# Attention banks, chunk order, spread sums and unread products in a fused two-layer kernel

## What is computed

```
h = concat(mean_over_hidden(x @ W.T + b), txt)           # 64 x 96 x 64
h = h + ssm_stack(ln(h))                                  # 4 state-space layers
h = h + ln_affine(z + moe(z)), z = ln(h)                  # 16 experts, top 2
h = h + attention(ln(h))                                  # 8 heads of 64, strictly causal
h = h + recurrent(ln(h))                                  # 96 steps, one after the other:
    i, f, o = sigmoid(x_t U + h V); g = tanh(...)
    c_new = h * c + i * g;  h_new = o * tanh(c_new)
```

## Time and profile before

| | us |
|---|---|
| three runs, median | 860.01 |
| lowest and highest of them | 848.58, 863.31 |
| the profiled execution, its own time | 853.76 |
| span of its instructions | 852.0 |
| mean granted TensorE clock in it | 0.854 of full |
| state-space part and before | 0 to 234 |
| expert slots 0 to 47, first attention | 234 to 404 |
| expert slots 48 to 95, steps 0 to 31 beside them | 404 to 556 |
| second attention | 556 to 714 |
| exposed steps 32 to 95 | 714 to 850 |

### The profile page before, as it was taken

One profiled execution on the slowest core, in us unless ns is written; L12 is line 12 of the kernel. 1 busy time (PEld: TensorE's weight loads), 2 busy tenths in 40 slices (PEclk: granted clock), 3 DMA queues, 4 the chain that ended last, 5 costly groups with the idle time before them and its releaser, 6 DMA issues.

```text
span 852.0 us, 16446 instructions
## 1 busy us (share of the span) xinstructions
PE 690.1 (81%) x6414; PEld 410.8 (48%) x6414; DVE 531.8 (62%) x1104; ACT 358.7 (42%) x667; POOL 253.6 (30%) x223
## 2 busy tenths in 40 slices
PE   3687888952689999988889999979899888776775
PEld 3674655642532222354234434357577666555554
DVE  3855675569956555375557867479767673556443
ACT  2232444333324455554444455635555434232332
POOL 4256764466400224120331402145223240011000
PEclk9999789866579999999989999979999979555555
DMA  9840000000044434101322222000000000000000
GB/s 185 140 77 10 1 1 2 1 0 1 0 138 132 134 107 140 39 2 33 95 73 79 84 88 79 18 2 2 2 2 2 1 2 5 7 11 7 11 9 12
DMA packets 42402, 36.85 MB, mean 43 GB/s; under 512 B 20888, under 2 KB 29848, under 8 KB 42328
## 3 DMA queue, kind: packets, MB, share of 16 engines
q1 hardware_dynamic: 41242, 35.57, 16.3%
q10 hardware_dynamic: 1088, 0.26, 0.2%
HBM read 33.85 MB, written 1.97 MB: 42 GB/s over the span
## 4 chain that ended last, share of the span: by engine, by line
PE 53%; DVE 25%; ACT 8%; issue 6%; POOL 4%; DMA 2%; SPq 1%; POOLq 0%; DVEq 0%; ACTq 0%
PE PS L1591 9%; PE PS L1578 8%; PE PS L1554 6%; PE PS L1626 3%; PE PS L1674 3%; PE PS L1685 3%; DVE XC L937 3%; PE PS L1605 2%; PE PS L1647 2%; PE PS L1540 2%; PE PS L1658 2%; DVE st L919 2%; DMA BIG<-in_x 2%; ACT Y L672 2%; DVE st L935 2%
## 5 line engine op out<-in xcount | busy, mean ns | idle before, releaser
L1591 PE MATMUL PS<-Y,W1f 64*128 64x512 f32 x384 | 110.1, 653 | 6.0 <-DVE Y L1078 3.9
L1578 PE MATMUL PS<-XC,w2s 128*64 128x512 f32 x384 | 104.1, 622 | 0.0
L1554 PE MATMUL PS<-LS,V 64*64 64x32 f32 x1140 | 70.3, 269 | 40.5 <-DVE LS L1214 40.5
L1554 PEld LDWEIGHTS PS<-LS,V 64*64 64x64 f32 x1140 | 58.3, 186 | 71.6 <-DVE LS L1214 65.2
L717 ACT ACTIVATE XC<-PS 128x1024 f32<-128x1024 f32 x68 | 69.3, 1022 | 54.0 <-PE PS L1578 45.3
L1078 DVE TENSOR_TENSOR Y<-XD,UF 128x512 f32<-128x512 f32 x96 | 64.8, 689 | 15.2 <-DMA UF<-gd 9.2
L574 POOL TENSOR_TENSOR Y<-XC 128x512 f32<-128x512 f32 x12 | 14.7, 1226 | 173.6 <-DVE XC L1058 173.6
L1591 PEld LDWEIGHTS PS<-Y,W1f 64*128 64x128 f32 x384 | 30.1, 188 | 50.9 <-DVE Y L1078 24.9
L1578 PEld LDWEIGHTS PS<-XC,w2s 128*64 128x64 f32 x384 | 19.2, 135 | 73.2 <-issue 62.2
L1201 DVE SCALAR_TENSOR_TENSOR LS<-LS 128x32 f32<-128x32 f32 x96 | 21.4, 222 | 51.3 <-ACT LS L812 39.4
L178 POOL TENSOR_TENSOR st<-st,mhalf 128x8 f32<-128x8 f32 x24 | 39.3, 1639 | 37.0 <-DVE st L922 37.0
(11 more groups left out here) (236 smaller groups left out, 1463.9 us busy)
## 6 DMA issues: line engine op xcount, KB each, us to landing
UF<-gd SPq DMA_DIRECT2D x192, 128.0 KB, 2.9
BIG<-in_x SPq DMA_DIRECT2D x8, 512.0 KB, 12.4
out<-X SPq DMA_DIRECT2D x48, 32.0 KB, 2.0
W1f<-in_L_ffn_w SPq DMA_DIRECT2D x2, 512.0 KB, 5.9
EX<-in_L_ffn_w SPq DMA_DIRECT2D x1, 1024.0 KB, 15.6
H<-in_txt SPq DMA_DIRECT2D x2, 256.0 KB, 12.6
w2s<-in_L_ffn_w SPq DMA_DIRECT2D x1, 512.0 KB, 9.9
gd<-EX SPq DMA_DIRECT2D x6, 64.0 KB, 1.7
```

What stands on the lines that cost most here:

```text
L1554: mm = pe.matmul(PS[r, b, o:o + HN], V3[r, g, :], HB[r, (t - 1) % 4, :], start=False, stop=True, skip_group_check=True)
L1578: mm = pe.matmul(PS[64 * h:64 * h + 64, 6, :], w2s[:, 2 * p + h, :], Hb[:, n % 2 * 2 + h, :], start=(p == 0), stop=(p == E // 2 - 1))
L1591: mm = pe.matmul(PS[:, n % 2 * 2 + h, :], W1f[r, 2 * p + h, :], Rb[r, n % 4, :], start=True, stop=True)
```

## The change

- Second attention: in range 2 the keys are turned into bank 5 (from its second unit on) and all Z go through bank 4, copied by ScalarE alone. `turn_keys` in bank 5 no longer waits for the queries' copies or for bank 7. TensorE's order within a unit changes: `turn_p` comes ahead of `project`, and range 2's two `queries` halves both come behind `gather`. VectorE's chunk work stands behind the unit's `less_max` and copies.
- Chunk 2's settling (all but its first half sum) comes seven slots later; `out` and what follows it one slot later for chunks 0 and 3 to 4. The recurrence and residual chunks 0 and 1 start earlier, by one and two slots.
- Squares go from GpSimd to ScalarE everywhere (TAIL_ACT in the second attention). In chunks 4 and 5 the scaling goes from GpSimd to VectorE.
- In exposed steps a residual chunk's parts are spread over twelve slots (XALONE) and the two sums of a half are parts of their own (r and q). In the second attention chunks 2 and 3 get new unit numbers.
- In each exposed step but the last and the six with `att_out` or `turn_x`, TensorE does one fp32 product of 256, 384, 160 or 256 columns by step number modulo 4, into bank 1. Nothing reads it and it waits for nothing; its operands are expert weights.

```diff
-        TAIL_DVE = {0: (2, 3, 4, 5), 1: (6, 7), 2: (8, 9), 3: (10,), 4: (11, 12), 6: (13, 14)}
-        TAIL_POOL = {0: ("sq0",), 1: ("pw0", "mu0", "ga"), 2: ("sq1",), 4: ("pw1", "mu1")}
+        TAIL_DVE = {0: (2, 3, 4, 5), 1: (6, 7), 2: (8, 9), 3: (10,), 4: (11, 12), 5: (13, 14)}
+        TAIL_POOL = {1: ("pw0", "mu0", "ga"), 4: ("pw1", "mu1")}
+        TAIL_ACT = {1: 0, 4: 1}
...
-        LS0 = 3 * E + 11
+        LS0 = 3 * E + 10
...
-                     sq1=9, k11=10, k12=10, pw1=10, mu1=11, out=12, t0=13, t1=13, k13=13, k14=13)
-
-        XB = (3 * E + 4, 3 * E + 15, None, None, NPR + 12, NPR + 28)
-        XLATER = dict(ao0=0, ao1=1, r0=0, r1=1, n0=1, n1=1, ones=2, sq=2, n2=3, n3=3, pw=3, mu=4, turn=5, c0=5, c1=5)
-        XU = {2: 12, 3: 18}
-        ULATER = dict(ao0=0, r0=0, ao1=1, r1=1, n0=1, n1=1, ones=2, sq=1, n2=2, n3=2, pw=2, mu=3, turn=4, c0=4, c1=4)
+                     sq1=9, k11=10, k12=10, pw1=10, mu1=11, out=13, t0=14, t1=14, k13=14, k14=14)
+
+        def settle_slot(j, p):
+            if j == 1 and p in ("out", "t0", "t1", "k13", "k14"):
+                return SB[j] + LATER[p] - 1
+            return SB[j] + LATER[p] + (7 if j == 2 and p not in ("s0", "k0", "k1") else 0)
+
+        XB = (3 * E + 2, 3 * E + 13, None, None, NPR + 12, NPR + 28)
+        XALONE = dict(ao0=0, r0=0, q0=1, ao1=2, r1=2, q1=3, n0=4, n1=5, sq=6, n2=7, n3=7, pw=7, ones=8, mu=9, turn=10, c0=10, c1=11)
+        XLATER = dict(ao0=0, ao1=1, r0=0, q0=0, r1=1, q1=1, n0=1, n1=1, ones=2, sq=2, n2=3, n3=3, pw=3, mu=4, turn=5, c0=5, c1=5)
+        XU = {2: dict(ao0=11, r0=11, q0=11, ao1=12, r1=12, q1=12, n0=13, n1=14, sq=14, n2=15, n3=15, pw=15, mu=15, ones=17, turn=19, c0=19, c1=19),
+              3: dict(ao0=16, r0=16, q0=16, ao1=20, r1=20, q1=20, n0=21, n1=22, sq=22, n2=23, n3=23, pw=23, mu=23, ones=24, turn=26, c0=26, c1=26)}
...
+            return [(c, p) for c in range(NC) for p in parts if XB[c] is not None and XB[c] + (XALONE if XB[c] >= NPR else XLATER)[p] == g]
...
+        JR2 = JOBS[[un[0] for un in UNITS].index(2)]
+
+        def z_bank(q):
+            return 4 if q >= JR2 else 4 + q % 2
+
+        def z_done(n):
+            return (min(n, JR2) + 1) // 2 + max(0, n - JR2), min(n, JR2) // 2
+
+        def key_bank(u):
+            return 5 if u and UNITS[u - 1][0] == 2 else 7
...
+            def squares(j, r):
+                act.wait_ge(S("ln_c"), ln_no(j, r))
+                act.activation(Ysqr[:, r, :, :], Ycen[:, r, :, :], ACT.Square).then_inc(S("ln_q"), 1)
+
+            def squares_x(c):
+                act.wait_ge(S("x_c"), c + 1)
+                act.activation(Xsqr, Xcen, ACT.Square).then_inc(S("x_q"), 1)
...
                     if x - 1 in us:
                         total(x - 1)
-                    for k in TAIL_DVE.get(x - 1 - us[0], ()):
-                        settle(NC - 1, k)
-                    for c, part in in_unit(x - 1 - us[0], "r0", "r1", "n0", "n1", "ones", "n2", "n3", "c1"):
-                        residual_part(c, part)
                     if x in us:
                         less_max(x)
                     for u in due(x, us, 0):
                         keys_out(u)
                     for u in due(x, us, 1):
                         z_out(u, 0)
+                    for k in TAIL_DVE.get(x - 1 - us[0], ()):
+                        settle(NC - 1, k)
+                    for c, part in in_unit(x - 1 - us[0], "r0", "q0", "r1", "q1", "n0", "n1", "ones", "n2", "n3", "c1"):
+                        residual_part(c, part)
...
+                if k == 4:
+                    dve.wait_ge(S("x_r"), c + 1)
+                    dve.wait_ge(S("x_tp"), c)
+                    dve.tensor_tensor(Xnrm, Xcen, st[:, 3, x_part()].unsqueeze(2).to_broadcast([128, CH, D]), ALU.mult).then_inc(S("x_o"), 1)
...
             def turn_keys(u, nU):
                 r, _, b0, n, w = UNITS[u][0:5]
-                pe.wait_ge(S("u_ev0"), nU)
                 pe.wait_ge(S("xt_ev"), u)
-                borrow()
+                if key_bank(u) == 7:
+                    pe.wait_ge(S("u_ev0"), nU)
+                    borrow()
+                else:
+                    pe.wait_ge(S("z_ev1"), z_done(JR2)[1])
...
+                    if r == 1 and 0 in nxt:
+                        queries(UNITS[x][1] + 1, 0, nU, nO, nX)
+                        nU += 1
+                    for u in due(x, us, 0):
+                        turn_p(u)
                     for u in due(x, us, 2):
                         if u != us[-1]:
                             project(UNITS[u][1], u, nU)
                             nO += 1
...
                     for u in due(x, us, 1):
                         gather(u, 0)
-                    if 1 in nxt:
-                        queries(UNITS[x][1] + 1, 1, nU, nO, nX)
-                        nU += 1
+                    for half in nxt:
+                        if r == 2 or half == 1:
+                            queries(UNITS[x][1] + 1, half, nU, nO, nX)
+                            nU += 1
...
+                if g >= LS1 and t < T - 1 and not residual(g, "ao0", "ao1", "turn"):
+                    n = (256, 384, 160, 256)[t % 4]
+                    pe.matmul(PS[:, 1, 0:n], W1f[:, 0, :], w2s[:, 0:8, :].rearrange("p e d -> p (e d)")[:, 0:n], start=True, stop=True)

```

More of the change, by code:

```diff
@@ L363, in in_unit @@
         def in_unit(i, *parts):
-            return [(c, p) for c in XU for p in parts if XU[c] + ULATER[p] == i]
+            return [(c, p) for c in XU for p in parts if XU[c][p] == i]
         def settling(g, *parts):
-            return [(j, p) for j in range(NC) for p in parts if SB[j] + LATER[p] == g and (j < NC - 1 or p in ("s0", "k0", "k1"))]
+            return [(j, p) for j in range(NC) for p in parts if settle_slot(j, p) == g and (j < NC - 1 or p in ("s0", "k0", "k1"))]
         def residual(g, *parts):
-            return [(c, p) for c in range(NC) for p in parts if XB[c] is not None and XB[c] + XLATER[p] == g]
+            return [(c, p) for c in range(NC) for p in parts if XB[c] is not None and XB[c] + (XALONE if XB[c] >= NPR else XLATER)[p] == g]
         def step_at(g):
@@ L624, in _ @@
                         ahead += 1
-                for c, part in residual(g, "sq", "pw", "mu"):
-                    normed(c, part)
-                for j, part in settling(g, "sq0", "pw0", "mu0", "ga", "sq1", "pw1", "mu1"):
+                for c, part in residual(g, "pw", "mu"):
+                    if part == "pw" or c not in (4, 5):
+                        normed(c, part)
+                for j, part in settling(g, "pw0", "mu0", "ga", "pw1", "mu1"):
                     settle(j, part)
@@ L734, in z_out @@
                     q = JOBS[u] + k
-                    if q % 2:
+                    if q % 2 and q < JR2:
                         continue
@@ L793, in attend @@
                         z_out(u, 0)
-                    if 1 in nxt:
-                        u_out(UNITS[x][1] + 1, 1)
+                    for half in nxt:
+                        if r == 2 or half == 1:
+                            u_out(UNITS[x][1] + 1, half)
+                    if x - us[0] in TAIL_ACT:
+                        squares(NC - 1, TAIL_ACT[x - us[0]])
+                    for c, part in in_unit(x - 1 - us[0], "sq"):
+                        squares_x(c)
                     if x == us[0] + 6:
@@ L839, in _ @@
                     gates_out(g - 9)
-                for c, part in residual(g, "c0"):
-                    copy_x(c)
-                for j, part in settling(g, "t0", "t1"):
-                    turned(j, int(part[1]))
+                for c, part in residual(g, "c0", "sq"):
+                    if part == "c0":
+                        copy_x(c)
+                    else:
+                        squares_x(c)
+                for j, part in settling(g, "sq0", "sq1", "t0", "t1"):
+                    if part[0] == "t":
+                        turned(j, int(part[1]))
+                    else:
+                        squares(j, int(part[2]))
                 for G, half in EARLY.get(g, ()):
@@ L1264, in _ @@
                     dve.wait_ge(S("b2a"), NC)
-                for c, part in residual(g, "r0", "r1", "n0", "n1", "ones", "n2", "n3", "c1"):
+                for c, part in residual(g, "r0", "q0", "r1", "q1", "n0", "n1", "ones", "n2", "n3", "mu", "c1"):
+                    if part == "mu":
+                        if c in (4, 5):
+                            norm(c, 4)
+                        continue
                     residual_part(c, part)
@@ L1667, in gather @@
                 for k in ks:
[L1668 to L1669 removed]
+                    q = JOBS[u] + k
+                    n0, n1 = z_done(q if q >= JR2 else max(0, q - 1))
+                    if q >= JR2 or q % 2 == 0:
+                        pe.wait_ge(S("z_ev0"), n0)
+                    if q == JR2 or q < JR2 and q % 2:
+                        pe.wait_ge(S("z_ev1"), n1)
                 for x in range(4):
@@ L1731, in attend @@
```

(7 more changed lines are left out.)

53 lines of the change are left out of this document (24 added, 29 removed).

## The result

The median after is 861.93 us (857.26 to 868.78, 20 runs), before it is 859.83 us (848.58 to 864.43, 20 runs). The ratio is 1.0088, 95% interval [1.0052, 1.0124]. The kernel is 2.1 us (0.2%) slower by the medians and 0.9% slower by the ratio, where 819 us was forecast. Medians and ranges in this document are over all runs; the ratios leave out runs more than 1.5% above the fastest of their kernel, which takes out the slowest of before's, as these spread over 1.9%.

The account below looks back on a forecast made before the run. Expert slots and second attention were taken as bound by TensorE, the exposed steps by latency. 853.8 - 13.9 (clock) - 7.0 (sums spread) - 5 (chunk later) - 9 (second attention) = 818.9 us, range 811 to 851.

Parts of the forecast that it names:

- I take it that it holds: Exposed steps: with the filler the high clock lasts from 720 us on, -13.9 us (bounds -14 to +18); chance 0.50.
- The filler's cover at the high clock: Exposed steps: at the high clock the wait for VectorE hides the filler, cost 0 (bounds 0 to +0.1 us a step).
- Rivals 1: Exposed steps: clock stays low despite the filler, steps 2.2 us on average against 1.92, +16 us, 847 in all; chance 0.33.
- Rival 2: Exposed steps: clock low, filler at its upper price (2.23 us a step, +18), other parts at lower ends, 865; chance 0.07.
- rival 3: Exposed steps: clock holds but falls in the six slots without filler, +10 us, 829 in all; chance 0.10.
- The rule on transposes: Six slots without filler: transposes don't count for the clock as products do; by it the 829 us case would come out.
- Sums of exposed steps spread, -7.0: Exposed steps: chunks 4 and 5 over twelve slots, square and scaling off GpSimd, -7.0 us (bounds -4 to -10).
- The remainder: Exposed steps: what chunk work still adds after spreading, 1.6 us a chunk, 3.2 for two.
- A chunk settled later, -5: Expert slots: moving chunk 2 seven slots and the square off GpSimd removes a 4.1 us wait, -5 us (bounds -7 to 0).
- Second attention, -9: Second attention: maximum and subtraction ahead of chunk work, plus freed banks, give -9 us (bounds -3 to -14).
- The fall of the clock at the end: End of the second attention: 10.2 us at low clock become some 6.5 at high clock, -3.7 us.
- chunk 3's end in the tail: Second attention, after the last unit: chunk 3 ends two units later where VectorE is idle, so hidden.

Follow-up runs that it names:

- e2: Kernel after with the unread products also in the six slots it leaves out, widths unchanged: 848.90 us, ratio 0.9888.
- e6: Kernel after with unread products in every exposed step but the last, 512 columns in steps 51, 52, 67 and 68: 829.61 us (826.84 to 875.12).
- e5: Kernel after with wider unread products (384, 512, 160, 320 columns; 512 in steps 51, 52, 67, 68), in every exposed step but the last: 828.28 us.
- e9: Kernel after with e5's widths and nothing else, the same six slots left out: 827.92 us (824.99 to 861.09), ratio 0.9640.
- e1: Kernel after without its 57 unread products, all else kept: 839.32 us, ratio 0.9816.
- e11: Kernel after with the wider unread products only from step 48 on: 836.03 us, ratio 0.9738.
- e3: Kernel after without unread products, chunks 4 and 5 back in six neighbouring slots: 846.30 us, ratio 0.9875.
- e10: e5 with chunks 4 and 5 back in six neighbouring slots: 837.47 us, ratio 0.9759.
- e7: Kernel after without unread products, the expert stage's slots as before the change: 841.48 us, ratio 0.9761.
- e4: Kernel before with VectorE's maximum and subtraction ahead of the chunk work in the second attention, nothing else: 880.84 us, ratio 1.0278.
- e8: The same kernel as e5, run six more times: 826.47 us, ratio 0.9639.

## Why the prediction was wrong, step by step

**The step that failed.** It is "I take it that it holds", the term of -13.9 us for the high clock in the exposed steps. The clock did not hold: it fell at 729.6 us, and the term came out as a loss, 148.6 us in the exposed steps with the filler against 126.2 without. The rows behind it (stretches at 1.00) have products of 512 columns nearly without a gap; I put a mixture with 264 columns a step beside them and weighed it as if it were closer to those than to the exposed steps. The change's widths lose the clock at 729.6 us (after) or 770.1 us (e2, every step filled); with 512 columns in four steps more it is lost at 717.3 us in one run and, by the mean granted clock, kept in three (e6). e5's widths, 344 columns on average, held it or won it back, with one partial loss in e9's four runs. That the question decides the forecast was right, and so was the size of the term once it holds: steps 33 to 95 take 107.8 us in e9 against 121.0 in e1, 13.2 us. The term took every fourth step at the high clock as 1.69 us too; it takes 1.75, and with that the sum is 13.0 and not 13.9. The filler's cover at the high clock (0 a step) held too: 1.68 to 1.70 us with it.

**The price when it doesn't hold.** Rivals 1 and 2 had the right mechanism and too low a price: 2.23 us a step, measured 2.52. Built up from the same blocks I had 2.43, 2.18, 2.27 and 2.04 us for steps whose hidden states come 2.67, 2.63, 2.44 and 2.36 apart. Most of the missing 0.2 to 0.45 lies at the filler: 256 columns take 732.78 - 731.62 = 1.16 us from their start to the next product, priced by passes at 0.84, and 512 take 755.61 - 753.60 = 2.01 in e11, where two passes are 1.68. So 0.3 us a product are missing whatever its width. I had named a weight load that isn't hidden, but only for the high clock and at 0.1. Rival 2 decides from 2.32 us with the rest at 23 us; the step went past that, and the rest was worth 20.5 us (22.6 less the 2.1 between the medians of after and before), or 22.5 by e1 against its own runs of before, a little less than 23. So the outcome lies between my rivals 1 (847) and 2 (865), nearer the second, which had 0.07.

**Where it fell.** The place was rival 3's: the first slots without filler. Its price (2 us for the four filled steps behind a slot, 829 in all) assumed that the clock comes back within them; with the change's widths it doesn't. The rule on transposes that I set beside it (the Trainium skill, TensorE: Matmul & The Clock Gate, Part 4) isn't needed for it, and no run tests it by itself: e9 has the same four transposes in the same six slots, with wide products around them, and the clock holds in three of four runs.

**Sums of exposed steps spread, -7.0.** About right. At the low clock the forecast was 9 for the spreading and the work off GpSimd together, and steps 33 to 95 take 129.0 - 121.0 = 8.0 us less in e1 than before, 6.0 of it from the spreading (e3 against e1; 7.0 by the medians). At the high clock the forecast was 7; e10 against e5 gives 9.2 for the spreading, with the two falls of the clock in it. The remainder was forecast as 1.6 us a chunk; at the low clock the two steps that stand out add 0.55 + 0.44 = 1.0 us.

**A chunk settled later, -5.** Less came out: the stage went from 151.7 to 150.1 us in the kernel after, 1.6 us, and e7 against e1 gives 2.2 by the medians. Executions of the old slots (before, e4, e7) take 151.7 to 156.1 us and of the new ones 150.1 to 152.8, so the size isn't fixed to better than some 2 us. The stall was removed as described (slot 57 takes 3.31 us instead of 7.29, and slots 56 to 63 together 24.2 instead of 30.8), but slots 64 to 71, where chunk 2 now meets the steps and residual chunk 1, take 32.8 instead of 27.0. I charged 1.5 us for that meeting; it costs 5.8.

**Second attention, -9.** The number looks right, 8.3 to 8.4 us in after, e5 and e9, but some 2 us of it come back in step 33: 6.0 to 6.5 us are left. Two steps of the reasoning failed. The fall of the clock at the end, for which I took off 3.7 us, stays, 6.8 us long instead of 10.2 and later. And chunk 3's end in the tail, which I called hidden, is not: TensorE waits 1.45 us for its copy, and the low clock lies behind it. I gave most of the gain to the order on VectorE and 2.5 us to the banks; by e4 a good part of that order alone costs 25 us, so that division has nothing behind it.

**The sum, with the clock held.** e9's profiled execution has a span of 825.7 us, 26.3 under before's 852.0: +1.1 ahead of slot 48, 0 in the expert slots, -6.0 up to step 33's hidden state, -21.2 in steps 33 to 95. Forecast were 34.9; of the missing 9 in this execution 5 are the chunk and 3 the attention, while the exposed steps gave the 20.9 forecast for them. With the clock held the time is near 828 us, inside the 811 to 831 that I gave for that case.

## What to carry to other kernels

Filler for the sake of the clock must be priced at the clock that you have if it fails: here it cost 22.6 us at the low clock and nothing at the high one, and a filler that held only part of the way (e2, 848.9 us) was worse than none (e1, 839.3). Size it with a margin (512, 384 and 320 columns instead of 256 cost an ordinary step at the high clock nothing), and test it by starting it late: the filler that brought the clock back in e11 also healed the two falls behind the stalls of e10. When an engine's order is changed, ask which bank the work now pushed back is holding: maximum and subtraction first were a loss of 25 us by themselves, through waits for bank 7. And end a stage's measurement behind its tail: the attention's gain was 8.3 us up to step 32 and 6.0 up to step 33.

## What the runs showed that I had not expected

- A TensorE that is recorded busy is not enough for its clock: 120.83 of 122.40 us busy at 0.50 to the end of the kernel after. The Trainium skill (TensorE: Matmul & The Clock Gate, Part 1) says that the hardware sets the clock by how busy the engine has been; busy as the profile records it doesn't carry that here, since TensorE, recorded busy 16.80 of 16.80 us, got its clock back with wider products in e11, and didn't at 16.00 of 16.00 us in e6.
- A fall isn't for good: with e5's widths it healed within 3.4 to 10.2 us (e8, e10, e11).
- Within one kernel the executions lie up to 48 us apart: 826.84 to 875.12 us in e6, at mean granted clocks of 0.918 and 0.840.
- An unread fp32 product of 256 columns takes 1.16 us of TensorE's time at the low clock, though two passes are 0.84; one of 512 takes 2.01, and two of its passes are 1.68.
